# A fused attention and FFN layer on eight cores: the mask multiply on POOL, and matmuls interleaved over PSUM banks in both FFN stages

## The reference

```python
x = x + _layernorm(_L0_attn_ref(_layernorm(x, axis=-1), Wq, Wk, Wv, Wo, bo), axis=-1)
x = x + _layernorm(_L0_ffn_ref(_layernorm(x, axis=-1), w1, w2, w3), axis=-1)

# attention: q, k with rope; scores masked by qi >= ki; softmax; times v; times Wo, plus bo
s = jnp.where(qi >= ki, s, -jnp.inf)
a = jax.nn.softmax(s, axis=-1)

# ffn
def _quantize(w):
    gamma = jnp.mean(jnp.abs(w))
    return jnp.clip(jnp.round(w / (gamma + EPS)), -1.0, 1.0)
hidden = sigmoid(x @ _quantize(w1).T) * (x @ _quantize(w2).T)
return hidden @ _quantize(w3).T
```

## Time and profile before

| | us |
|---|---|
| median of 3 runs | 5805.48 |
| their range | 5751.69 to 5839.08 |
| the profiled execution | 5747.44 |
| its span, slowest core | 5745.9 |
| spans of the eight cores | 5712.1 to 5745.9 |
| PE busy (matmul) | 2774.3 |
| DVE busy | 2299.4 |
| ACT busy | 915.5 |
| POOL busy | 271.9 |

### The profile page before, as it was taken

The page is one execution under the profiler, slowest core; times in us unless marked ns, Lnnn a source line. Parts: engine busy times, 40 slices in busy tenths (PEclk is TensorE's granted clock), DMA queues, the critical chain, the costliest instruction groups (busy, mean ns, idle before and its releaser), DMA issues.

```text
span 5745.9 us, 36911 instructions; the slowest of 8 cores (5712.1 to 5745.9 us)
## 1 busy us (share of the span) xinstructions
PE 2774.3 (48%) x11251; PEld 1084.6 (19%) x11251; DVE 2299.4 (40%) x3047; ACT 915.5 (16%) x1158; POOL 271.9 (5%) x518
## 2 busy tenths in 40 slices
PE   1555555555555532222222222666477767665564
PEld 1111111111111111111111111112222323222221
DVE  5222222222222234444444443003545454557777
ACT  1222222222222211111111111441100000000001
POOL 0000000000000001111111110000000000000000
PEclk9776666667766655555555555558688888877777
DMA  5211111111111033333333332004122222222221
GB/s 118 45 21 24 29 26 20 20 20 24 24 29 23 7 68 76 79 78 79 79 82 82 80 77 50 0 0 117 44 95 95 95 95 95 91 92 75 95 87 73
DMA packets 107475, 346.77 MB, mean 60 GB/s; under 512 B 12432, under 2 KB 69904, under 8 KB 78480
## 3 DMA queue, kind: packets, MB, share of 16 engines
q0 software_dynamic: 74016, 107.77, 12.9%
q1 hardware_dynamic: 17712, 123.38, 5.9%
q10 hardware_dynamic: 15552, 113.25, 5.5%
HBM read 443.71 MB, written 8.39 MB: 79 GB/s over the span
## 4 chain that ended last, share of the span: by engine, by line
PE 44%; DVE 25%; DMA 12%; ACT 10%; issue 8%; DVEq 1%; ACTq 0%; POOL 0%; POOLq 0%; SPq 0%
DMA AB<-w_t 10%; ACT MID L472 8%; PE pSA L895 7%; PE pSB L895 5%; DVE STT L281 4%; DVE STT L299 4%; PE pSA L455 3%; PE pAVB L502 3%; PE pAVB L395 3%; PE pSA L976 3%; PE pT L346 3%; PE pSA L395 3%; PE pSB L976 2%; PE pG L521 2%; PE pSA L672 2%
## 5 line engine op out<-in xcount | busy, mean ns | idle before, releaser
L346 PE MATMUL pT<-IDE,MID 128*128 128x128 bf16 x1216 | 153.8, 307 | 1227.7 <-DVE MID L325 1150.0
L281 DVE TENSOR_REDUCE STT<-AB 128x1 f32<-128x704 bf16 x384 | 340.2, 886 | 504.4 <-DMA AB<-w_t 490.7
L895 PE MATMUL pSA<-MID,WQS 128*128 128x512 bf16 x1408 | 396.5, 452 | 283.6 <-DVE WQS L878 283.6
L472 ACT ACTIVATE MID<-pSA,BIA 128x1024 bf16<-128x1024 f32 x212 | 236.0, 1113 | 1085.2 <-PE pSB L455 1085.2
L502 PE MATMUL pAVA<-MID,AB 128*65 128x512 bf16 x424 | 210.4, 597 | 353.3 <-ACT MID L472 207.9
L346 PEld LDWEIGHTS pT<-IDE,MID 128*128 128x128 bf16 x1216 | 117.7, 138 | 1260.7 <-issue 1260.7
L480 DVE TENSOR_TENSOR MID<-MID,AUX 128x1024 bf16<-128x1024 bf16 x128 | 88.6, 692 | 622.9 <-ACT MID L472 622.7
L895 PE MATMUL pSB<-MID,WQS 128*128 128x512 bf16 x1408 | 311.1, 379 | 0.0
L976 PE MATMUL pSA<-WQS,AB 128*128 128x512 bf16 x576 | 170.7, 428 | 278.3 <-DVE AUX L955 222.5
L455 PE MATMUL pSA<-MID 64*128 64x512 bf16 x300 | 151.9, 608 | 307.0 <-DVE STT L288 289.3
L279 POOL DMA_DIRECT2D AB<-w_t x384 | 203.0, 529 | 1815.3 <-DVE STT L288 1763.3
(11 more groups left out here) (136 smaller groups left out, 4019.4 us busy)
## 6 DMA issues: line engine op xcount, KB each, us to landing
AB<-w_t POOLq DMA_DIRECT2D x384, 176.0 KB, 3.3
AUX<-w_t ACTq DMA_DIRECT2D x66, 1024.0 KB, 4.8
XS<-w_t SPq DMA_DIRECT2D x66, 1024.0 KB, 4.8
MID<-x_glob SPq DMA_DIRECT2D x36, 1024.0 KB, 6.1
XS<-x_glob ACTq DMA_DIRECT2D x36, 1024.0 KB, 4.8
WQS<-wq_t POOLq DMA_DIRECT2D x16, 512.0 KB, 5.9
WQS<-wk_t POOLq DMA_DIRECT2D x15, 512.0 KB, 5.0
WQS<-wv_t POOLq DMA_DIRECT2D x15, 512.0 KB, 5.2
```

The lines of the kernel that those rows point to most:

```text
L281: em("V", lambda e, par=par: e.tensor_reduce(ACOL, absbuf(par), AX.X, ALU.add, apply_absolute_value=True))
L346: tok = em("T", lambda e, dc=dc, k=k: e.transpose(pT[:, k * 128:(k + 1) * 128], XLT[:, dc * 128:(dc + 1) * 128], IDE[:]), "T" if k == 7 el ...
L472: e.activation(expsl(hb, 0, par), pbuf[:], AF.Exp, bias=b, scale=0.125),
L895: e.matmul(pbank[:, th * 512:(th + 1) * 512], w12q(m, qpar)[:, dc * 128:(dc + 1) * 128], xln2(dc, th * 512, (th + 1) * 512), start=(dc == ...
```

## The change

There are three edits. The mask multiply of the attention goes from DVE's list to POOL's, with a semaphore `GC` of its own that PE waits for. In the first FFN stage the two loops over `th` and `dc` change places: each slice of weights is used for both halves, one after the other, and only the very last matmul raises PE's semaphore; sigmoids or products follow in a loop of their own. In the second FFN stage the loops over `hs` and the tiles of the group change places in the same way: PE waits for all four banks first, uses each slice of the hidden units for the four banks in turn, and raises its semaphore once per chunk; the four additions on DVE follow.

```diff
-        for k in ("C", "C2", "X0", "X1", "CG0", "CG1", "W0", "W1", "W2", "W3",
+        for k in ("C", "C2", "GC", "X0", "X1", "CG0", "CG1", "W0", "W1",
+                  "W2", "W3",
...
                         if m is not None:
-                            wt("V", "A", ta)
-                            tv = em("V", lambda e, hb=hb, par=par, m=m:
+                            wt("G", "A", ta)
+                            tv = em("G", lambda e, hb=hb, par=par, m=m:
                                     e.tensor_tensor(expsl(hb, 1, par),
                                                     expsl(hb, 0, par), m,
-                                                    ALU.mult), "V")
-                            e_tok[(hb, qc, i)] = (tv, "V", 1)
-                            last_exp[hb] = (tv, "V")
+                                                    ALU.mult), "GC")
+                            e_tok[(hb, qc, i)] = (tv, "GC", 1)
+                            last_exp[hb] = (tv, "GC")
...
-                for th in range(2):
-                    psum_wait([pkeys[th]])
-                    tok = None
-                    for dc in range(NDC):
+                psum_wait([pkeys[0], pkeys[1]])
+                tok = None
+                for dc in range(NDC):
+                    for th in range(2):
                         tok = em("T", lambda e, dc=dc, m=m, th=th, qpar=qpar,
...
-                                 "T" if dc == NDC - 1 else None)
+                                 "T" if (dc == NDC - 1 and th == 1) else None)
+                for th in range(2):
                     if m == 0:
                         wt("A", "T", tok)
...
-                for hs in range(4):
-                    pb, pk = pbank4[hs]
-                    psum_wait([pk])
-                    wt("T", "V", t_q6)
-                    tok = None
-                    for g, j in enumerate(range(j0, j1)):
-                        wt("T", "V", hid_tok[j])
+                psum_wait(["pSA0", "pSA1", "pSB0", "pSB1"])
+                wt("T", "V", t_q6)
+                tok = None
+                for g, j in enumerate(range(j0, j1)):
+                    wt("T", "V", hid_tok[j])
+                    for hs in range(4):
+                        pb = pbank4[hs][0]
                         tok = em("T", lambda e, g=g, j=j, tc=tc, hs=hs,
...
-                                 "T" if j == j1 - 1 else None)
+                                 "T" if (j == j1 - 1 and hs == 3)
+                                 else None)
+                for hs in range(4):
+                    pb, pk = pbank4[hs]
                     wt("V", "T", tok)
```

## The result

The changed kernel takes 6283.2 us (median of 10 runs, 6236.8 to 6342.6), the kernel before takes 5754.8 us on the same chip (10 runs). The ratio is 1.088, with an interval of 1.082 to 1.094. The forecast was 6305 us in a range of 6150 to 6450.

What follows compares the result with a forecast made beforehand. No engine was full, so successive waits bound the kernel. 165 + 77 + 222 + 67 = 531 us on the profiled 5747.4 gave 6278; going halfway to the median gave 6305 us, range 6150 to 6450.

Steps and rivals of the forecast that it cites:

- Masks: Attention: two masks in a row on POOL lengthen each masked step, 165 us in sum, between 0 and 299.
- P: Attention: duration of one mask multiply on POOL, taken as 2.29 us, between 0.69 and 3.34.
- Rival (a): Attention: POOL is quick, a mask takes 1.15 us, masks cost 19 us, 6132 us in all; chance 0.12.
- First FFN stage: Both halves finish together, so a second product and a longer clock restart per tile: 77 us, from 13 to 86.
- The second product: First FFN stage: both products now follow PE's end, adding 0.80 us to the path in each of 44 tiles.
- The clock's term: First FFN stage: after the longer pause a restart costs 2.90 us instead of 1.94, in 44 tiles.
- Second FFN stage: Four banks fill and drain as one: 222 us of pauses plus 67 us of clock.
- The pauses: Second FFN stage: PE stands 3.57 us at each of 56 boundaries, with group ends and ninth group 222 us.
- The clock's share: Second FFN stage: about half a clock restart, 1.2 us, at each of 56 boundaries: 67 us, between 0 and 236.
- Rival (b): Second FFN stage: the clock stays low throughout, 236 us instead of 67, 6447 us in all; chance 0.12.
- Rival (c): Both FFN stages: reused weights are not loaded again, matmul spacing falls, so the kernel is not slower; chance 0.02.
- The 27 us added for the median: Whole kernel: the median of runs lay 58 us above the profiled execution; the forecast went half that way.

Runs made afterwards that it cites:

- e1: Only the attention masks moved to POOL, both FFN stages as in the kernel before: 5996.5 us, ratio 1.017.
- e9: Kernel before with only the first FFN stage's halves interleaved, plus 28 matmuls of no use behind each tile: 5732.9 us, ratio 0.995.
- e8: Kernel before plus 28 matmuls of no use behind each tile of the first FFN stage: 5752.4 us, ratio 0.984.
- e5b: Second run of the kernel before with only the four-bank second FFN stage, plus 14 matmuls of no use behind each chunk: 6077.1 us.
- e7: Kernel before with DVE quantizing the first FFN stage's weights a tile ahead: 5394.7 us, ratio 0.933.
- e4: Kernel before with the second FFN stage interleaved over two banks at a time instead of four: 5780.5 us, ratio 0.999.
- e6: Kernel before with only the first half's mask on POOL, the second's left on DVE: 5843.7 us, one run.

## Why the prediction was right, and which terms were off

**What bounds the kernel.** The forecast priced each edit in its own stage from the wait that ends last there. Three separate kernels give 499 us where the whole change makes 497, so the stages were indeed independent.

**Masks: forecast 165 us, measured 144.** The mechanism held: POOL's two masks run one behind the other and the second one ends the step. Two sizes were off, both on the high side. P is 2.11 us and not 2.29, which alone gives 34 x 2.43 + 30 x 1.97 = 142. And there is no pause of 0.11 us between POOL's two masks: the row of two takes 4.18 us, slightly less than twice 2.11. A masked step has grown by 2.26 us (7.74 less 5.48), and the last step of a block by 1.79 (7.73 less 5.94 up to PE's next matmul), its 0.47 us less being the cover that the forecast had at 0.46. That gives 34 x 2.26 + 30 x 1.79 = 131 us, and the attention shows it: over all 16 pairs it takes 1364 us where it took 1234 (medians of the undisturbed cores, eight of the changed kernel and e1, 58 of the kernels with both masks on DVE). The other 13 us of the 144 lie outside the attention, mostly in the projections and in the keys and values of all tokens. They are no more than the spread of kernels whose code there is the same: the 14 later projections take 872 to 889 us on the 58 cores and 880 to 889 on the eight. So no cost outside the attention is shown, and the masks were priced 34 us too high, not 21. That P came so close was in part luck, since 2.29 was a choice between 0.69 and 3.34. The estimate from the Trainium skill's GPSIMD Engine Reference, Performance versus the Vector engine, was P = 2.25; the trace's 2.11 is 6% below it. Rival (a), with P at 1.15, fell by the row of 2.11.

**First FFN stage: forecast 77 us, measured 68.** The two terms were each off, in opposite directions. The second product was put at 0.80 us a tile, which is 35 us. It measures 0.90 by the pause (7.28 less 6.38), 0.89 by the waits ((323.3 - 284.3) / 44) and 0.90 by e9 less e8, so 39 us. The second product itself is 0.80 us, as forecast. The other 0.10 lies between the end of the last quantizing pass and PE's first matmul, 0.36 us in e9 (4507.27 to 4507.63) and 0.26 in e8 (4500.74 to 4501.00); PE now waits there for both halves' banks, but no run shows that this is the cause. The clock's term was put at 44 x (2.90 - 1.94) = 42 and measures 28 by the filled kernels and 27 by the rows: on core 4 the first blocks cost 44 x 2.52 more than the second ones after, and 44 x 1.90 before. The step that was too high is "a longer pause gives the clock no reason to rise sooner, so I take 2.90": after the longer pause a restart costs 2.52 us in the mean, so it rose by 0.6 us and not by 0.96.

**Second FFN stage: forecast 289 us, measured 282.** The pauses were worked out at 222 us (3.57 a boundary, 19 at the ends of groups, 2.4 in the ninth; they add up to 221), and measure 224: 3.56 a boundary in e5b, and 18.8 at the groups' ends in the list of waits (242.5 less 223.7). The clock's share was a choice between 0 and 236 us, 67 was taken and 58 measured. The reason given, half a restart at every boundary, is not what the rows show. The clock falls in 35 of the 56 chunks behind such a pause (core 4), in those shown within a microsecond of PE's return, and each such chunk is then 1.7 us longer (9.55 us from start to start against 7.87). That makes 35 x 1.68 = 59 us, the 58 measured, and 1.05 a boundary, close to the 1.2 charged, but the agreement of these two numbers was luck. Rival (b), a clock that stays low, fell by the chunk of 5367.16, all at 1.00, and by the 58 us.

**Rival (c), weights not loaded again.** PEld counts 11251 loads before and after, and pairs that share a slice are 0.216 us apart, as those that don't. The Trainium skill's figure of 131 ns sustained at 512 columns (TensorE: Matmul & The Clock Gate, Back-to-back issue gap) is not what the traces show: e7's first FFN stage, in which PE never stands, has 928 matmuls in 200 us, 216 ns each. The saving of 126 ns a matmul did not exist.

**The sum.** The edits were put at 531 us and measure 497 on die 1 (494 by the stages): 21 too much for the masks by the stages, 9 and 7 for the FFN stages. That the medians stand 528 us apart is therefore no confirmation to the microsecond. The missing 30 us or so belong to executions like the profiled one, whose die 0, with the 0.81, is 59 us longer than die 1 (6282.1 and 6223.1). The forecast knew nothing of it, and it made up for the terms that were put too high. The 27 us added for the median were not needed for this comparison either: the kernel before has its median at 5754.8 in it, 7 above its profiled execution. In the runs beside the experiments its median lies at 5783 to 5802, so where it falls is itself uncertain by more than these 27 us.

## What to carry to other kernels

Read what a loop's order does to the moment when a buffer becomes free, not how often an operand is used in a row: with one bank always filling while another is emptied the order was free (e4), and with all four in step it cost 224 us of pauses and 58 us of clock. An operation moved to an idle but slower engine costs its full difference if it is a link of the chain; how idle its old engine was says nothing. Two of them one behind the other on the slow engine cost about twice what one did (131 us in the attention and 144 ahead of the FFN, against 76 to 81 in e6). Where a trace shows PE waiting for the same engine once per tile, look first for work that this engine could have done a tile earlier: that was worth 367 us here, where holding the clock without it was worth 79.

## What the runs showed of the hardware that was not expected

- VectorE's mask took 1.43 us beside one on POOL and 0.69 alone, and POOL's stayed at 2.11; VectorE's ended 0.55 us after POOL's in all 64 steps (e6, core 4).
- After a pause of 3.40 us between chunks PE resumed at 2.4 GHz in the chunks shown and fell to 1.2 GHz within the next microsecond in two of the three, and came back within the same chunk; 35 of 56 chunks on core 4 had such a stretch. A fast start after a pause doesn't mean that the clock is kept.
- Matmuls of no use held the clock at 1.00 and made the kernel before faster, 0.984 (0.981 to 0.987): the stage fell from 1011 to 932 us, though PE had 28 matmuls more in each tile.
- A granted clock of 0.81, beside 0.50 and 1.00, in some executions and not in others: on the four cores of die 0 in the changed kernel's profiled one, on all eight in e1's, in different stages. What sets it is not shown. One of its stretches, core 2 of the changed kernel:

```profile
4527.50:4544.50 17.00, 13.91 (x52) 5.55 (x52) 2.57 (x4) 1.19 (x2) 0.00 (x0) 0.81 0.18 63
```

- Left open: whether the masks on POOL cost anything outside the attention, since the 13 us seen there lie within the spread of the same code; and what the 9 us are that two banks at a time still cost (e4).
